# A state-space and expert-routing kernel on one core: the last mixer batch is projected in two parts, and the last layer's rows are gathered with an add

## The chip, the cores and the metric

One core of a Trainium2 chip runs the whole program. The metric is the device time of one execution in microseconds (us). Five engines run instruction streams of their own and meet at semaphores: TensorE (PE), VectorE (DVE), ScalarE (ACT), GpSimd (POOL) and SyncE (SP). The two that issue DMAs here are SP (plain copies) and POOL (gathers by an index, and copies that add into their destination). All of them share the core's 16 DMA engines.

## What is computed

Three layers over x of 8 batches x 2048 tokens x 256 features, all in fp32 (the biases, weights and index tables are left out here):

```
x = x + 0.5 * ffn(layernorm(x))      # first expert layer
x = x + mixer(layernorm(x))          # state-space layer
x = x + 0.5 * ffn(layernorm(x))      # last expert layer
# ffn: gate by 8 Sinkhorn rounds, each of 8 experts takes its 256 best tokens,
#      out[token] = gate * x[token] @ W_expert; of several experts the highest-numbered stands
# mixer: xr = x @ W_in.T; x_conv = silu(conv4(xr[:512])); delta = softplus(x_conv)
#      h[t] = exp(-delta * A) * h[t-1] + x_conv^2      (16 states for each of 512 channels)
#      y = x_conv * sum(h) * silu(xr[512:]) + D * x_conv;   out = y @ W_out.T
```

## The kernel before, in words

The program has four stages: `route` (normalise the rows of x, gates, top 256 tokens), `mixer`, `route` again on the mixer's result, and `ffn`. The first expert layer is computed inside `mixer`, one batch ahead of the state-space layer.

**`mixer`.** Channels go in four units of 128 (J = 4), each with 16 states (N = 16), so that a batch has 64 steps q = 0 to 63. At a step ACT makes the decay exp(delta * neg_a) in a state buffer (L1341), DVE scans it over 2048 tokens (L1143), and after each odd step POOL issues a DMA that adds the even step's state into the odd one's (L1034). PE then sums the pair into four PSUM banks `ps_sum` through an identity matmul (L1555), sixteen states in eight pairs. When a unit's eight pairs are in, DVE multiplies the sum with the gate (`gate`, L1116) and forms the unit's y (`combine`, L1124). The output projection y @ W_out.T (`project_out`, L1523) needs all four units. For a batch b it runs in eight pieces r, spread over the steps of batch b + 1: PE projects 2 x 128 tokens over the four units into a PSUM bank, ACT copies it to a `rows_out` buffer (`copy_out`, L1275), and POOL adds it to x2 in HBM by DMA (`add_result`, L1018), 256 KB each. For the last batch there is no next one to hide it: after all scans the eight pieces run one after the other. SP waits for all adds (the waits on `x2_added`), and only then does the second `route` start.

**`ffn`.** A batch is sixteen slots (`SL` = 16; two per expert, 128 tokens each). For a slot POOL gathers 128 normalised rows (`f_picked`, L1716), PE turns them (L1798), DVE copies them out of PSUM (L1754), PE applies the expert (L1805), ACT scales by the gate (L1784), and SP stores the result to `routed_rows` (L1690). When all sixteen slots of batch m are stored, POOL gathers the result back in token order, sixteen gathers of 128 rows (`f_back`, L1728), and DVE adds each into `total[m % 2]`, which holds the batch's x (L1769). SP stores `total` to the output (L1697) and loads x of a later batch into it (`load_x`, L1683). The order of the work is written out in "rounds" b of slots s. Each engine takes round b, slot s in turn, and the lags are constants:

```
NX = NY = NK = 8
BRING, JOIN, LOAD = SL + 6, SL + 10, 3
if s == LOAD and there(b - 1) and there(b - 3):          # SP: wait out_stored, then load_x(b - 1)
if s == JOIN - SL + 2 and there(b - 2):                  # SP: wait added, then store out of b - 2
m, t = behind(b, s, BRING)                               # POOL: gather back t of batch m, 22 slots after slot t
m, t = behind(b, s, JOIN)                                # DVE: add gather t, 26 slots after slot t; at t == 0 wait x_in
```

So in round b POOL starts the gathers back of batch b - 1 behind the pick of slot 6, SP loads the x of batch b - 1 once slot 3 of round b is scaled and stored, and DVE first needs that x at slot 10. Each ring has eight buffers: POOL's pick of slot s waits until slot s - 8 is turned, its gather back t until DVE has added t - 8, ACT's scaling until the store eight slots before has landed. The x of batches 0 and 1 is loaded at the start of the stage.

## Time and profile before

| | us |
|---|---|
| median of 3 runs | 3737.79 (3731.17 to 3739.79) |
| the profiled execution, its time | 3728.65 |
| its span | 3727.1 |
| DVE busy in the span | 3116.6 (84%) |
| PE busy | 2784.6 (75%) |
| ACT busy | 2123.0 (57%) |
| POOL busy | 1322.5 (35%) |
| granted PE clock, mean | 0.86 |

Busy shares are of the whole span. The stages have different limits: the mixer, to about 2950 us, keeps DVE at its scans, and the last expert layer, from about 3316 us, has no engine that is busy all the time. So the places are read one by one: the stretch between the last scan and the second `route`, and the rounds of the last layer.

### The profile page before, as it was taken

The page shows a single profiled execution, that of the slowest core. Times are in us where ns is not written, and L with a number is a line of the kernel's source. Part 1 is how long each engine was busy: PE and PEld are TensorE (multiplying, and loading weights), DVE is VectorE, ACT ScalarE, POOL GpSimd, SP SyncE. Part 2 cuts the span into 40 slices and gives each one's busy share as a digit, 9 for nine tenths or more (in the row PEclk, how much of TensorE's full clock was granted, in tenths as well). Part 3 has the DMA queues.
Part 4 walks back from the last instruction along what each step waited for, and adds up shares of the span by engine and source line. Part 5 has one row for each costly group of instructions (what it writes and reads, how often), then busy time and mean ns, then how long its engine had stood idle before and what let it go on. Part 6 is the DMA issues. An engine that isn't in the chain of part 4 may idle for free. (4 is left out here: it accounts for less than half of the span.)

```text
span 3727.1 us, 29733 instructions
## 1 busy us (share of the span) xinstructions
PE 2784.6 (75%) x9244; PEld 1530.2 (41%) x9244; DVE 3116.6 (84%) x2640; ACT 2123.0 (57%) x2277; POOL 1322.5 (35%) x897
## 2 busy tenths in 40 slices
PE   8703688899889799889988978987896687025653
PEld 4502333354345346435434534633442445024442
DVE  6797579999999999999999999999999566982222
ACT  6301467876877877787687787777767263001111
POOL 0002254436345344443734534450111100025665
PEclk9655799999999999999999989999998896557776
DMA  7202277688678778868867878886776462034666
GB/s 275 105 0 85 72 179 178 145 181 183 150 163 168 174 173 167 183 145 182 185 150 162 167 170 173 169 178 121 141 144 123 86 257 108 0 109 130 224 219 243
DMA packets 146619, 574.71 MB, mean 154 GB/s; under 512 B 22144, under 2 KB 73920, under 8 KB 99776
## 3 DMA queue, kind: packets, MB, share of 16 engines
q0 software_dynamic: 77136, 399.56, 51.6%
q1 hardware_dynamic: 69360, 173.68, 12.7%
q8 instruction: 55, 0.90, 0.1%
q14 instruction: 68, 0.56, 0.0%
HBM read 154.72 MB, written 117.51 MB: 73 GB/s over the span
## 5 line engine op out<-in xcount | busy, mean ns | idle before, releaser
L1143 DVE TENSOR_TENSOR_SCAN state<-state,drive 128x2048 f32<-128x2048 f32 x512 | 2224.3, 4404 | 54.0 <-ACT state L1341 53.7
L1341 ACT ACTIVATE state<-delta,neg_a 128x2048 f32<-128x2048 f32 x512 | 1019.4, 2005 | 230.3 <-DMA state<-state 95.7
L1555 PE MATMUL ps_states<-state,ident 128*128 128x512 f32 x1800 | 856.4, 621 | 109.5 <-DMA state<-state 94.8
L1034 POOL DMA_DIRECT2D state<-state x256 | 234.9, 919 | 1314.1 <-DVE state L1143 1303.7
L1491 PE MATMUL ps_proj<-x1t,w_in 128*128 128x512 f32 x1024 | 505.0, 637 | 90.6 <-ACT xc L1290 32.3
L1555 PEld LDWEIGHTS ps_states<-state,ident 128*128 128x128 f32 x1800 | 348.7, 200 | 516.5 <-issue 385.5
L1507 PE MATMUL ps_proj<-conv_in,tap 128*128 128x512 f32 x1024 | 488.1, 628 | 53.9 <-ACT conv_in L1262 33.0
L982 POOL DMA_INDIRECT picked<-normed_rows,slot_now x112 | 355.9, 3178 | 99.1 <-PE ps_rows L1472 55.0
L998 POOL DMA_INDIRECT x<-routed_rows,row_now x112 | 345.3, 3083 | 34.6 <-issue 34.6
L1491 PEld LDWEIGHTS ps_proj<-x1t,w_in 128*128 128x128 f32 x1024 | 202.8, 203 | 369.6 <-issue 265.8
L1507 PEld LDWEIGHTS ps_proj<-conv_in,tap 128*128 128x128 f32 x1024 | 203.8, 202 | 319.2 <-issue 280.3
L1754 DVE COPY f_picked_t<-f_ps_turn 128x256 f32<-128x256 f32 x128 | 54.1, 424 | 258.2 <-DMA picked<-normed_rows,slot_now 115.3
L1805 PE MATMUL f_ps_out<-f_expert,f_picked_t 128*128 128x256 f32 x512 | 184.5, 499 | 91.1 <-DVE f_picked_t L1754 55.2
L1784 ACT ACTIVATE f_routed<-f_ps_out,slot_gate 128x256 f32<-128x256 f32 x128 | 60.4, 474 | 316.8 <-PE f_ps_out L1805 136.1
L1523 PE MATMUL ps_rows<-w_out,xc 128*128 128x256 f32 x768 | 204.6, 391 | 5.0 <-DVE xc L1124 5.0
L1716 POOL DMA_INDIRECT f_picked<-normed_rows,f_slot_now x128 | 131.2, 1025 | 199.1 <-issue 189.1
L1523 PEld LDWEIGHTS ps_rows<-w_out,xc 128*128 128x128 f32 x768 | 188.6, 306 | 19.6 <-issue 7.2
L1269 ACT COPY delta<-ps_proj 128x512 f32<-128x512 f32 x124 | 72.1, 583 | 213.3 <-PE ps_proj L1507 213.2
L1805 PEld LDWEIGHTS f_ps_out<-f_expert,f_picked_t 128*128 128x128 f32 x512 | 118.6, 255 | 117.9 <-DVE f_picked_t L1754 61.7
L1728 POOL DMA_INDIRECT f_back<-routed_rows,f_row_now x128 | 122.5, 957 | 101.2 <-DVE f_total L1769 53.3
L1464 PE MATMUL ps_rows<-expert,picked_t 128*128 128x256 f32 x448 | 116.1, 382 | 5.0 <-ACT picked_t L1227 5.0
L1275 ACT COPY rows_out<-ps_rows 128x512 f32<-128x512 f32 x64 | 37.6, 587 | 136.7 <-PE ps_rows L1523 124.3
(288 smaller groups left out, 3233.9 us busy)
## 6 DMA issues: line engine op xcount, KB each, us to landing
state<-state POOLq DMA_DIRECT2D x256, 1024.0 KB, 7.1
delta<-xc POOLq DMA_DIRECT2D x24, 1024.0 KB
normed_rows<-rows_in SPq DMA_DIRECT2D x8, 2048.0 KB
x_rows<-x SPq DMA_DIRECT2D x16, 1024.0 KB, 7.4
x_rows<-rows_out POOLq DMA_DIRECT2D x64, 256.0 KB, 8.3
normed_rows<-rows_mid SPq DMA_DIRECT2D x8, 2048.0 KB
f_total<-x_rows SPq DMA_DIRECT2D x8, 2048.0 KB
routed_rows<-f_routed SPq DMA_DIRECT2D x128, 128.0 KB
```

Source lines behind the costliest of these rows:

```text
L982: nc.gpsimd.indirect_dma_start(out=picked[s % NX][:], out_offset=None, in_=g.normed, in_offset=bass.IndirectOffsetOnAxis(ap=slot_now[:, s: ...
L998: nc.gpsimd.indirect_dma_start(out=x1[:, t, :], out_offset=None, in_=g.routed[0], in_offset=bass.IndirectOffsetOnAxis(ap=row_now[:, t:t + ...
L1034: nc.gpsimd.dma_start(out=state[held(q)][:], in_=state[held(q - 1)][:], accum_op=ALU.add).then_inc(pair_landed(b, q // 2)[0], 16)
L1143: nc.vector.tensor_tensor_scan(state[held(q)][:], state[held(q)][:], drive[j % 2][:], 0.0, ALU.mult, ALU.add).then_inc(state_ready, 1)
L1341: nc.scalar.activation(state[held(q)][:], delta[j % 2][:], ACT.Exp, scale=g.neg_a[:, j, n:n + 1]).then_inc(decay_ready, 1)
L1491: mm = nc.tensor.matmul(ps_proj[bank][:], g.w_in[:, k, col:col + P], x1t[:, k, c * CH:(c + 1) * CH], start=(k == 0), stop=(k == KD - 1))
L1507: mm = nc.tensor.matmul(ps_proj[c % 2][:], tap[:, j * KC + k, :], conv_in[:, c * CH + k:c * CH + k + CH], start=(k == 0), stop=(k == KC - 1))
L1523: mm = nc.tensor.matmul(out_bank(r, last)[:, (t % 2) * D:(t % 2 + 1) * D], y_now[j].rearrange("p (n t) -> p n t", t=T)[:, :, t], g.w_out[: ...
L1555: mm = nc.tensor.matmul(ps_sum[c][:], g.ident[:], state[held(q)][:, c * CH:(c + 1) * CH], start=(opening and n == 1), stop=(n == N - 1))
L1716: nc.gpsimd.indirect_dma_start(out=picked[s % NX][:], out_offset=None, in_=g.normed, in_offset=bass.IndirectOffsetOnAxis(ap=slot_now[b % 2 ...
L1728: nc.gpsimd.indirect_dma_start(out=back[t % NK][:], out_offset=None, in_=g.routed[m], in_offset=bass.IndirectOffsetOnAxis(ap=row_now[m % 2 ...
L1805: mm = nc.tensor.matmul(ps_out[s % NT4][:, 0:D], picked_t[s % NT4][:, k, :], expert[:, s // NH, k, :], start=(k == 0), stop=(k == KD - 1))
```

## The change

There are two parts, in two stages.

**Mixer, last batch only.** The eight pieces of the output projection are done in two parts. Pieces k = 0 to 7 project units 0 to 2 during the fourth unit's steps (PE at steps 55, 57, 59 and 61, ACT's copies at 59, 61, 62 and 63, into `x1`), and POOL adds them to x2 in two DMAs of 1 MB (`add_first_units`, behind steps 61 and 63). Pieces 8 to 15 project unit 3 alone after the scans, are copied into the two `delta` buffers, and are added by four DMAs of 512 KB (`add_last_unit`). The last pair of states is not added by DMA any more: PE sums the states of steps 62 and 63 each by itself (`add_state`), and DVE's last `gate` begins bank by bank.

**Last expert layer.** The gather back adds into `total` by itself (`compute_op=ALU.add`), so DVE's add and the `back` buffers are gone. POOL waits for x (`x_in`) at gather 0 of a batch, and the wait for `added` is gone. The rings for picks and results have sixteen buffers. SP's store of the output moves from slot 12 to slot 10 of its round and waits for the gathers.

The diff, cut to its core:

```diff
@@ mixer @@
+    END = NB - 1
+    END_PUT = {55: (0, 1, 2), 57: (3, 4), 59: (5, 6), 61: (7,)}
+    END_COPY = {59: (0, 1), 61: (2,), 62: (3,), 63: (4, 5, 6, 7)}
+    END_ADD = {61: 0, 63: 1}
...
         for i in range(NOUT):
-            sp.wait_ge(x2_added[i], NB * 16 * (GO // NOUT))
+            sp.wait_ge(x2_added[i], (NB - 1) * 16 * (GO // NOUT))
+        sp.wait_ge(end_out, 4 * 16)
...
+        def add_first_units(i):
+
+            pool.wait_ge(x1_stored[0], NB * 16)
+            pool.wait_ge(x1_stored[1], NB * 16)
+            pool.wait_ge(end_copied, (i + 1) * G2 // 2)
+            pool.sem_inc(g.passed_pool, 1)
+            nc.gpsimd.dma_start(out=x2_v[END, :, i * TH:(i + 1) * TH, :], in_=x1[:, i * TH:(i + 1) * TH, :],
+                                accum_op=ALU.add).then_inc(end_added[i], 16)
+
+        def add_last_unit(i):
+
+            pool.wait_ge(end_added[i // 2], 16)
+            pool.wait_ge(end_copied, G2 + 2 * (i + 1))
+            pool.sem_inc(g.passed_pool, 1)
+            nc.gpsimd.dma_start(out=x2_v[END, :, 4 * i:4 * i + 4, :],
+                                in_=delta[i // 2][:, i % 2 * 4 * D:(i % 2 + 1) * 4 * D].rearrange("p (t d) -> p t d", t=4),
+                                accum_op=ALU.add).then_inc(end_out, 16)
...
             for q in range(1, J * N, 2):
-                pool.wait_ge(state_ready, b * J * N + q + 1)
...
+                if not last or q < J * N - 1:
+                    pool.wait_ge(state_ready, b * J * N + q + 1)
...
+                if last and q in END_ADD:
+                    add_first_units(END_ADD[q])
...
         batches(pool, body)
-        for i in range(GO):
-            add_result(NB - 1, i)
+        for i in range(4):
+            add_last_unit(i)
...
         def gate(b, j):
-            dve.wait_ge(pair_used, sums_taken(b, (j + 1) * (N // 2) - 1))
+            last = isinstance(b, int) and u == NB * J - 1
+            if not last:
+                dve.wait_ge(pair_used, sums_taken(b, (j + 1) * (N // 2) - 1))
             dve.wait_ge(res_gated, u + 1)
             for c in range(C):
+                if last:
+                    dve.wait_ge(end_summed, c + 1)
...
+        def copy_end(k):
+            if k == 0:
+                act.wait_ge(x1_stored[0], NB * 16)
+                act.wait_ge(x1_stored[1], NB * 16)
+            act.wait_ge(end_done, k + 1)
+            nc.scalar.copy(end_rows(k), ps_rows[1 - k % 2][:]).then_inc(end_copied, 1)
...
+        def add_state(q):
+            pe.wait_ge(state_ready, END * J * N + q + 1)
+            for c in range(C):
+                mm = nc.tensor.matmul(ps_sum[c][:], g.ident[:], state[held(q)][:, c * CH:(c + 1) * CH],
+                                      start=False, stop=(q == J * N - 1))
...
+        def project_end(k):
+            if k == 0:
+                pe.wait_ge(y_done, END * J + 3)
...
+            if k == G2:
+                pe.wait_ge(y_done, END * J + 4)
+            pe.wait_ge(end_copied, count(k - 1))
+            r, units = k % G2, (range(J - 1) if k < G2 else (J - 1,))
...
+                    if last:
+                        for r in END_PUT.get(q, ()):
+                            project_end(r)
+                        if q == J * N - 3:
+                            add_state(q + 1)
+                        if q == J * N - 1:
+                            add_state(q)
+                            continue
@@ ffn @@
-    NX = NY = NK = 8
+    NX = NY = SL
...
-    BRING, JOIN, LOAD = SL + 6, SL + 10, 3
+    BRING, STORE, LOAD = SL + 6, SL + 10, 3
...
-                if s == JOIN - SL + 2 and there(b - 2):
-                    sp.wait_ge(added, (b - 1) * T)
+                if s == STORE - SL and there(b - 2):
+                    sp.wait_ge(joined[b % 2], b // 2 * 16 * T)
...
                     if t == 0:
                         pool.wait_ge(rows_set, m + 1)
+                        pool.wait_ge(x_in[m % 2], (m // 2 + 1) * 16)
                         for k in range(NY):
                             pool.wait_ge(routed_out[k], (m + 1) * 16 * (SL // NY))
-                    pool.wait_ge(added, count(m * T + t - NK + 1))
...
-                        out=back[t % NK][:], out_offset=None, in_=g.routed[m],
+                        out=total[m % 2][:, t, :], out_offset=None, in_=g.routed[m],
...
+                        compute_op=ALU.add).then_inc(joined[m % 2], 16)
...
-                m, t = behind(b, s, JOIN)
-                if there(m):
-                    if t == 0:
-                        dve.wait_ge(x_in[m % 2], (m // 2 + 1) * 16)
-                    dve.wait_ge(back_in[t % NK], (m * (T // NK) + t // NK + 1) * 16)
-                    nc.vector.tensor_tensor(total[m % 2][:, t, :], total[m % 2][:, t, :], back[t % NK][:], ALU.add
```

How the change moves instructions at the end of the mixer, on PE. Before, from the fourth unit's opening to the first projections of the last batch (L1546 opens the sums, L1555 sums a pair, L1523 projects; a row's x counts like matmuls in a row):

```order
L1546 MATMUL ps_states<-ones 128x512 x4
L1555 MATMUL ps_states<-state,ident 128x512 x28
L1523 MATMUL ps_rows<-w_out,xc 128x256
L1523 MATMUL ps_rows<-w_out,res 128x256
L1523 MATMUL ps_rows<-w_out,xc 128x256 x3
```

And now, the last part of the same stretch (L1586 is `project_end`, L1639 sums a pair, L1569 is `add_state`):

```order
L1639 MATMUL ps_states<-state,ident 128x512 x4
L1586 MATMUL ps_rows<-w_out,xc 128x256
L1586 MATMUL ps_rows<-w_out,res 128x256
L1586 MATMUL ps_rows<-w_out,xc 128x256 x2
L1586 MATMUL ps_rows<-w_out,res 128x256
L1586 MATMUL ps_rows<-w_out,xc 128x256
L1569 MATMUL ps_states<-state,ident 128x512 x4
L1639 MATMUL ps_states<-state,ident 128x512 x4
L1569 MATMUL ps_states<-state,ident 128x512 x4
L1586 MATMUL ps_rows<-w_out,xc 128x256 x16
```

Three quarters of the projection stand before the last sums, and sixteen matmuls of 256 columns are left behind them instead of 64.

In the last layer, SP's order of issues, before (L1690 stores a slot, L1683 loads x, L1697 stores the output):

```order
L1690 DMA routed_rows<-f_routed 128x256 x45
L1697 DMA out<-f_total 128x4096
L1690 DMA routed_rows<-f_routed 128x256 x7
L1683 DMA f_total<-x_rows 128x4096
L1690 DMA routed_rows<-f_routed 128x256 x9
```

And now:

```order
L1773 DMA routed_rows<-f_routed 128x256 x43
L1780 DMA out<-f_total 128x4096
L1773 DMA routed_rows<-f_routed 128x256 x9
L1766 DMA f_total<-x_rows 128x4096
L1773 DMA routed_rows<-f_routed 128x256 x7
```

The store of the output comes two slots earlier. The load of x stays where it was, behind the store of slot 3, while its first user is now POOL behind the pick of slot 6.

## Rows read from the trace of the kernel before

**Rows 1.** Busy time by stretch at the mixer's end (x: instructions; PEclk: granted clock).
```profile
2920.00:2931.00 11.00, 4.38 (x9) 1.94 (x10) 11.00 (x3) 0.00 (x0) 0.85 (x1) 0.96 0.54 109
2945.00:2988.00 43.00, 30.92 (x128) 29.69 (x128) 4.18 (x5) 4.69 (x8) 6.84 (x8) 0.88 0.35 49
```
**Rows 2.** Timeline of DVE, last unit (start, us, what, idle before and releaser).
```profile
2892.42 38.94 DVE L1143 TENSOR_TENSOR_SCAN state<-state,drive 128x2048 f32<-128x2048 f32 x9
2944.35 2.48 DVE L1116 TENSOR_TENSOR xc<-ps_states,xc 128x512 f32<-128x512 f32 x4 [12.99 <-PE ps_states L1555]
2946.87 2.35 DVE L1124 SCALAR_TENSOR_TENSOR xc<-xc,skip 128x2048 f32<-128x2048 f32 x1
```
**Rows 3.** Timeline of PE, last sums and first projection (durations at two clocks).
```profile
2893.73 3.70 PE L1555 MATMUL ps_states<-state,ident 128*128 128x512 f32 x8 [2.95 <-DMA state<-state]
...
2938.91 5.40 PE L1555 MATMUL ps_states<-state,ident 128*128 128x512 f32 x8 [3.36 <-DMA state<-state]
2949.28 1.23 PE L1523 MATMUL ps_rows<-w_out,xc 128*128 128x256 f32 x2 [4.96 <-DVE xc L1124]
```
**Rows 4.** Timeline of ACT, the last piece's copy.
```profile
2980.24 0.59 ACT L1275 COPY rows_out<-ps_rows 128x512 f32<-128x512 f32 x1 [2.98 <-PE ps_rows L1523]
```
**Rows 5.** Timeline of all engines where the mixer ends and `route` starts.
```profile
2981.50 0.86 POOL L1018 DMA_DIRECT2D x_rows<-rows_out  x1 [2.81 <-ACT rows_out L1275]
2988.11 1.76 SPq L221 DMA_DIRECT2D rows_mid<-x_rows  x4
```
**Rows 6.** DMA issues from 2940 to 2990 us (KB each, median us to landing).
```profile
x_rows<-rows_out POOLq DMA_DIRECT2D x8, 256.0 KB, 4.1
```
**Rows 7.** Busy time by stretch of the last layer, cut at each batch's first gather back.
```profile
3366.10:3414.00 47.90, 28.39 (x108) 20.97 (x106) 10.99 (x31) 7.95 (x17) 30.37 (x33) 0.71 0.47 132
...
3652.90:3697.70 44.80, 20.48 (x74) 15.52 (x74) 12.54 (x35) 6.53 (x14) 23.90 (x25) 0.74 0.67 219
3697.70:3727.10 29.40, 0.00 (x0) 0.00 (x0) 6.79 (x17) 0.00 (x0) 15.51 (x16) 0.50 0.70 274
```
**Rows 8.** Timeline of POOL, one round: the picks of slots 3 and 6, gathers back.
```profile
3497.70 0.94 POOL L1716 DMA_INDIRECT f_picked<-normed_rows,f_slot_now x1 [0.30 <-issue]
...
3505.22 0.95 POOL L1716 DMA_INDIRECT f_picked<-normed_rows,f_slot_now x1 [0.30 <-issue]
3510.59 0.95 POOL L1728 DMA_INDIRECT f_back<-routed_rows,f_row_now x1 [4.42 <-DVE f_total L1769]
```
**Rows 9.** Groups of POOL's instructions, 3366 to 3698 us (idle before, releasers).
```profile
L1728 POOL DMA_INDIRECT f_back<-routed_rows,f_row_now x113 | 107.9, 955 | 96.3 <-DVE f_total L1769 53.3 <-issue 32.9 <-PE f_ps_turn L1798 5.0
```
**Rows 10.** Timeline of SP in the last layer (SPq: its DMA queue).
```profile
3514.50 0.43 SPq L1683 DMA_DIRECT2D f_total<-x_rows  x1
...
3606.88 0.42 SPq L1683 DMA_DIRECT2D f_total<-x_rows  x1
...
3694.31 0.33 SPq L1683 DMA_DIRECT2D f_total<-x_rows  x1
3698.28 22.44 SPq L1697 DMA_DIRECT2D out<-f_total  x2
```
**Rows 11.** Chain of waits, two gathers of picks, start and us to landing.
```profile
3415.21 2.94 DMA f_picked<-normed_rows,f_slot_now
...
3514.35 8.04 DMA f_picked<-normed_rows,f_slot_now
```
**Rows 12.** Timeline of PE, one slot's expert matmuls and one turn.
```profile
3525.93 1.91 PE L1805 MATMUL f_ps_out<-f_expert,f_picked_t 128*128 128x256 f32 x4
3527.64 0.63 PE L1798 MATMUL f_ps_turn<-ident,f_picked 128*128 128x128 f32 x2
```
**Rows 13.** Busy time by stretch while the x of a batch is loaded.
```profile
3612.00:3614.00 2.00, 0.00 (x0) 0.00 (x0) 0.76 (x2) 0.00 (x0) 1.63 (x2) 0.50 1.03 418
3616.00:3618.00 2.00, 1.89 (x6) 1.62 (x7) 0.00 (x0) 0.47 (x1) 1.39 (x2) 0.50 0.72 270
```
**Rows 14.** Timeline of DVE, the first add of batch 7.
```profile
3705.53 0.43 DVE L1769 TENSOR_TENSOR f_total<-f_total,f_back 128x256 f32<-128x256 f32 x1 [7.28 <-DMA f_back<-routed_rows,f_row_now]
```

More of the change, by code:

```diff
@@ L796, in mixer @@
     x2_added = [sem(f"x2_added{i}") for i in range(NOUT)]
+    end_done, end_copied, end_summed, end_out = (sem(n) for n in ("end_done", "end_copied", "end_summed", "end_out"))
+    end_added = [sem(f"end_added{i}") for i in range(2)]
     x_v = x.rearrange("b (p t) d -> b p t d", t=T)
@@ L1031, in body @@
             for q in range(1, J * N, 2):
-                pool.wait_ge(state_ready, b * J * N + q + 1)
-                pool.sem_inc(g.passed_pool, 1)
-                nc.gpsimd.dma_start(out=state[held(q)][:], in_=state[held(q - 1)][:], accum_op=ALU.add
-                                    ).then_inc(pair_landed(b, q // 2)[0], 16)
+                if not last or q < J * N - 1:
+                    pool.wait_ge(state_ready, b * J * N + q + 1)
+                    pool.sem_inc(g.passed_pool, 1)
+                    nc.gpsimd.dma_start(out=state[held(q)][:], in_=state[held(q - 1)][:], accum_op=ALU.add
+                                        ).then_inc(pair_landed(b, q // 2)[0], 16)
+                if last and q in END_ADD:
+                    add_first_units(END_ADD[q])
                 for r in range(G2):
@@ L1352, in body @@
                         decay(b, q, first)
+                    if last:
+                        for k in END_COPY.get(q, ()):
+                            copy_end(k)
                     if n == BEGIN[j] and (j or not first):
@@ L1644, in ffn @@
     routed = [sb(f"f_routed{i}", [P, D]) for i in range(NY)]
-    back = [sb(f"f_back{i}", [P, D]) for i in range(NK)]
     total = [sb(f"f_total{i}", [P, T, D]) for i in range(2)]
@@ L1651, in ffn @@
     routed_out = [sem(f"f_routed_out{i}") for i in range(NY)]
-    back_in = [sem(f"f_back_in{i}") for i in range(NK)]
+    joined = [sem(f"f_joined{i}") for i in range(2)]
     x_in = [sem(f"f_x_in{i}") for i in range(2)]
     out_stored = [sem(f"f_out_stored{i}") for i in range(2)]
-    turned, copied, product, scaled, added = (
-        sem(n) for n in ("f_turned", "f_copied", "f_product", "f_scaled", "f_added"))
+    turned, copied, product, scaled = (
+        sem(n) for n in ("f_turned", "f_copied", "f_product", "f_scaled"))
     table = RankTable(ints=[sb(f"f_token_i{i}", [P, R * NH], I32)[:] for i in range(2)],
@@ L1743, in set_rows @@
         def set_rows(b):
-            for k in range(NK):
-                dve.wait_ge(back_in[k], count((b - 1) * 16 * (T // NK)))
+            if b >= 2:
+                dve.wait_ge(joined[b % 2], b // 2 * 16 * T)
             nc.vector.tensor_copy(row_now[b % 2][:], g.token_row[:, b, :]
```

24 lines of the change are left out of this document (19 added, 5 removed).

## The prediction

> **What bounds the kernel now.** The profiled execution took 3728.65 us over a span of 3727.1 and lies 9 us under the median of the runs, 3737.79. I make the sum against that execution and carry the difference over to the median. I read the busy times by stretch first, then the timelines at the two places that the change touches.
>
> *The mixer's end.* DVE scans without a gap to 2931.36 [rows 2]. Then it waits 13 us: the last pair is added by DMA, PE sums it from 2938.91 to 2944.31, DVE gates for 2.48 and combines for 2.35, and PE projects from 2949.28 [rows 2, 3]. The eight pieces take 3.57 each (a 0.59 copy and 2.98 of waiting for PE [rows 4]). POOL issues the last add at 2981.50, it lands in about 4.1, and `route` starts at 2988.11 [rows 5, 6]. So 57 us lie between the last scan and the next stage with nothing beside them, and every microsecond cut there is a microsecond of the total.
>
> *The last layer.* No engine is always busy: in the stretch from 3652.9 to 3697.7 PE works 20.5 of 44.8 us, POOL 23.9, and DMA has a share of 0.67 [rows 7]. POOL is the nearest to a bound, since a gather costs it 0.95 and the next starts 1.25 later [rows 8]: 32 gathers make 40.1 us a batch. From the first gather back of batch 0 (3366.1) to that of batch 7 (3697.7) it took 331.6 us for seven batches, 47.4 each [rows 7]. The difference is mostly POOL waiting for DVE's add to free one of eight buffers, 53.3 us in all [rows 9], 4.42 in the round shown [rows 8].
>
> **The mixer's end, part by part.** A sum of a pair (eight instructions) costs PE 3.70 at full clock and 5.40 at the lower one [rows 3]. A piece of 16 instructions takes 3.57, so one instruction 0.223. The first-part pieces have 12 (2.7), the second-part pieces 4 (0.9). From the end of the sum at 2897.4 [rows 3] PE now has eight first-part pieces (21.4) and six sums (pairs 27 to 30, and states 62 and 63 singly; 22.2): it is done at 2941.0, after the last scan. That is 3.3 before 2944.31. The gate now runs bank by bank beside the last sum, so only its last quarter (0.6) is left of 2.48, another 1.9. This is 5.2 in all. At the lower clock the six sums would cost 10 more. The clock granted there was 0.96 [rows 1] and PE will be fuller, so I take 1 off: 4.2 earlier, and the second part starts at about 2945.1.
>
> What are the scans' risks? ACT's eight new copies (0.59 each) stand behind decays of steps 59 to 63, which ACT makes well ahead of DVE. PE's sums come later by some pieces, and the decay of step 63 needs the sum of pair 27, now at about 2909.5, while its scan is due at 2927. I charge nothing. If that cover were gone, each late scan would cost what it is late by. The two adds of 1 MB go out behind the last state add and before the second part. They cost the path nothing unless they delay the last pair, which PE takes up only after a first-part piece and a sum.
>
> The second part is eight pieces of 0.9 (7.2), with adds of 512 KB after each two. The adds are what is late next. DMA engines moved adds of 8 KB per partition at 109 GB/s with a share of 0.54, 202 GB/s when busy, and adds of 2 KB at 49 with 0.35, 140 GB/s [rows 1]. These adds have 4 KB, between the two: 185 GB/s, 2.8 us each, bounds 2.6 and 3.7. The first is issued after two pieces and a copy, at 2947.8. Four transfers take 11.2, and the rest of a landing is 2.2 (4.1 less 1.9 for 256 KB at 140 [rows 6]): 2961.2. `route` follows 2.5 after the landing, as before (2981.50 + 4.1 to 2988.11 [rows 5, 6]): 2963.7 in place of 2988.1. **Gain 24.4**, between 18 (slow adds, PE at the lower clock) and 27.
>
> The Trainium skill (DMA: Bandwidth & Descriptors, Anatomy of one DMA) fits any POOL-issued DMA by 2.0 us + bytes at 436 GB/s, without a dearer case for adds. By that figure four adds would take 4.8 us, less than PE's pace, and the end would come 3 us sooner. The rows show adds at under half that rate, so they decide.
>
> **The last layer, part by part.** DVE's 128 adds and POOL's waits for them go: 53.3 us of POOL's idle time. What takes their place is the wait for x. SP loads the x of batch b - 1 in round b, behind slot 3's store. DVE needed it at slot 10, but POOL now wants it behind the pick of slot 6, and everything on POOL is queued behind that wait, so picks stop and then PE. In the round shown the pick of slot 3 was issued at 3497.70, that of slot 6 at 3505.22, and the load of x only at 3514.50 [rows 8, 10]: POOL would stand there before the load has even been issued.
>
> So a batch's period is now a loop. From a first gather back to the next round's pick of slot 3 POOL issues 25 gathers: 31.3 us. Then slot 3 must be scaled. PE turns slot 4 first, so: 2.5 until that pick, 2.9 for its landing on quiet queues [rows 11], 0.6 turn, 1.9 expert [rows 12], 0.6 scaling (at most a copy of twice the size [rows 4]) and 0.3 of hand-overs, 8.8. A burst of 2 MB makes picks late (8.04 beside the load issued at 3514.50, against 2.94 [rows 10, 11]). The store of the output is such a burst, some slots earlier in the round, and I add 1.9 for what is left of it: 10.7. Two issues by SP: 0.9. The landing of 2 MB: the load issued at 3606.88 kept the DMA engines full until about 3616.5, 9.6 us, beside gathers [rows 10, 13]. The last store of 2 MB, alone, took 6.4 (3720.72 to the end at 3727.1 [rows 7, 10]). With POOL standing still the load is nearly alone: 7.8. With 0.3 to wake POOL the period is 31.3 + 10.7 + 0.9 + 7.8 + 0.3 = **51.0**, against 47.4.
>
> This holds for five of the seven periods. The x of batch 1 is there from the start, so the first is POOL's own 40.1. In the last, no picks follow: 21.3 to the pick of slot 15, 11 to its scaling beside a burst, 0.9, and 9.5 to the landing, as the output store follows at once (11.2 with one beside it in the trace, 3694.31 to 3705.53 [rows 10, 14]): 43. Sum 40.1 + 255 + 43 = 338.1 against 331.6, **6.5 lost**, and 0.7 at the end, where a gather that adds lands later but DVE's last add of 0.43 goes.
>
> The gathers that add have no row. For POOL's time the bounds are a gather, 0.95, and half again as much, 1.4; a direct add costs it 0.86 [rows 5], less than a gather, so I take 0.95. For the DMA engines: at 140 to 185 GB/s the adds of a batch take 11 to 15 us and the rest some 23 (load, store, slot stores and picks), under 51, so they do not bind. The rings of sixteen add nothing by themselves: once POOL stops at slot 6 it cannot be more than seven picks ahead. SP's store of the output, now at slot 10, waits for gathers that POOL issued by slot 5, and costs nothing. The second `route` and the other layers are untouched.
>
> **Sum.** -24.4 + 6.5 + 0.7 = -17.2: 3711 for an execution like the profiled one, and 3737.8 - 17.2 = **3721** for the median.
>
> **The rivals.** (a) *The wait for x is much longer, and the kernel is slower.* In the trace slot 3 took 16.8 from its pick to the load (3497.70 to 3514.50). If that stays, with 9.5 for the landing, the period is 58.8 and the layer loses 40.1 + 294 + 45 - 331.6 = 47.5 more: 3738 - 24 + 48 = 3762. It decides from a period of 55. For it speaks the measured row; against it that part of those 16.8 is backlog of bursts, which empties while POOL stands still. 0.13. The Trainium skill (DMA: Bandwidth & Descriptors, Rules for kernel authors) says that an accumulating DMA must wait for the earlier DMA on the same bytes, so this wait cannot simply be dropped. By that rule the time is (a)'s or mine, according to the load.
> (b) *Between.* A period of 53 to 56 eats the mixer's gain: within 7.5 of the median. 0.12.
> (c) *The loop is short.* No backlog (8.8) and 6.8 for a load alone: period 48.1, 14.5 better than forecast: 3706. With the mixer's upper end, 3703. 0.10.
> (d) *The gathers do not add at a gather's price.* At 1.4 on POOL 13 of the 25 gathers cost 0.45 more, 6 us a period, 41 in all: 3762 too. 0.05.
> (e) *The mixer's end gives only 18*, by slow adds or late scans: 3727. This is inside my own case.
>
> **How the numbers follow.** 0.60 for the forecast (3708 to 3730), 0.10 for (c), 0.12 for (b), 0.18 for (a) and (d). About 0.2%, 7.5 us, is what a measurement of this kernel can tell from no change. Faster takes the first two and a sliver of (b): 0.72. Same 0.11, slower 0.17. The range leaves out the far half of (a) and (d) and the far end of (c): 3702 to 3748.
>
> **What would show it.** `route`'s first load at about 2964; PE's second part from 2945; scans as dense as before; the first x-wait of POOL at batch 2, 8 to 14 us long each, five times; no DVE add; gathers that add at 0.95 on POOL; distances of 40 once, then 51. A period under 45 or an `x_in` wait that is missing makes the second half of the argument wrong; a first load after 2972 the first.

## The result, and the profile after

The changed kernel took **3791.28 us** (median of 4 runs, 3786.41 to 3795.9) beside 3734.48 us for the kernel before (4 runs, 3729.42 to 3739.79). The ratio is 1.0155, 95% interval 1.0133 to 1.0177: 57 us slower. Forecast were 3721 us and a range up to 3748. The profiled execution took 3795.9 us over a span of 3794.0, the highest of the four, while that of the kernel before (3728.65) was below all of its runs; so the two spans are 66.9 us apart and the medians 57.

| part of the span, us | before | after | difference |
|---|---|---|---|
| start to the end of the last scan | 2931.4 | 2938.6 | +7.3 |
| last scan to the first load of the second `route` | 56.7 | 34.1 | -22.7 |
| from there to the first pick of the last layer | 328.0 | 327.6 | -0.4 |
| first pick to the first gather back | 50.0 | 59.9 | +9.9 |
| seven periods, first gather back of batch 0 to that of batch 7 | 331.6 | 395.6 | +64.0 |
| from there to the end | 29.4 | 38.2 | +8.8 |

The first line is no effect of the change. The stretch is the same but for the last batch's end, and in the 18 traces of the runs below, of kernels that differ only behind it or only in this end, it ended anywhere from 2920 to 2940 us.

**The mixer's end.** Timeline of DVE, last unit:

```profile
2899.69 38.94 DVE L1182 TENSOR_TENSOR_SCAN state<-state,drive 128x2048 f32<-128x2048 f32 x9
2945.51 1.48 DVE L1155 TENSOR_TENSOR xc<-ps_states,xc 128x512 f32<-128x512 f32 x2 [6.88 <-PE ps_states L1569]
...
2948.01 0.69 DVE L1155 TENSOR_TENSOR xc<-ps_states,xc 128x512 f32<-128x512 f32 x1 [0.17 <-PE ps_states L1569]
2948.74 2.35 DVE L1163 SCALAR_TENSOR_TENSOR xc<-xc,skip 128x2048 f32<-128x2048 f32 x1
```

The nine scans last 38.94 us without a gap, exactly as in [rows 2]: the copies and the sums held up none. DVE's wait behind them is 6.9 us, before 13. On PE the sums of state 62, pair 30 and state 63 stand back to back at a granted clock of 1.00, and after DVE's combine 32 matmuls are left:

```profile
2937.51 3.60 PE L1569 MATMUL ps_states<-state,ident 128*128 128x512 f32 x8
2940.95 3.60 PE L1639 MATMUL ps_states<-state,ident 128*128 128x512 f32 x8
2944.38 3.60 PE L1569 MATMUL ps_states<-state,ident 128*128 128x512 f32 x8
2951.15 9.41 PE L1586 MATMUL ps_rows<-w_out,xc 128*128 128x256 f32 x32 [3.17 <-DVE xc L1163]
```

Timelines of POOL and SP, from the first of the four adds to `route`'s first load:

```profile
2955.88 0.86 POOL L1049 DMA_DIRECT2D x_rows<-delta  x1 [16.03 <-ACT delta L1323]
...
2961.75 0.86 POOL L1049 DMA_DIRECT2D x_rows<-delta  x1 [1.07 <-issue]
...
2972.69 1.76 SPq L221 DMA_DIRECT2D rows_mid<-x_rows  x4
```

**The last layer.** Busy time by stretch, the first period, the second, and the end (they answer to [rows 7]; behind the length come the busy times of PE, of PE's weight loads, of DVE, ACT and POOL, each with its number of instructions, then the granted clock, the busy share of the DMA engines and GB/s):

```profile
3360.20:3410.50 50.30, 33.98 (x109) 22.60 (x108) 7.97 (x21) 8.81 (x19) 40.52 (x33) 0.68 0.62 131
3410.50:3470.00 59.50, 35.44 (x106) 23.16 (x104) 7.78 (x20) 8.52 (x18) 40.46 (x33) 0.61 0.71 185
...
3755.80:3794.00 38.20, 0.00 (x0) 0.00 (x0) 0.00 (x0) 0.00 (x0) 24.65 (x16) 0.50 0.66 165
```

POOL now works 40.5 us in a period, where it worked 30.4 [rows 7]. One round on POOL's timeline (compare [rows 8]): the first gather back of batch 1 and the pick behind it, then the picks of slots 3 and 6 of the next round, the gather that waits for x, and the one that waits in the round after:

```profile
3410.49 1.55 POOL L1811 DMA_INDIRECT f_total<-routed_rows,f_row_now  x1 [0.30 <-issue]
3412.34 0.98 POOL L1799 DMA_INDIRECT f_picked<-normed_rows,f_slot_now  x1 [0.31 <-issue]
...
3450.01 0.98 POOL L1799 DMA_INDIRECT f_picked<-normed_rows,f_slot_now  x1 [0.30 <-issue]
...
3459.41 0.98 POOL L1799 DMA_INDIRECT f_picked<-normed_rows,f_slot_now  x1 [0.30 <-issue]
3469.99 1.55 POOL L1811 DMA_INDIRECT f_total<-routed_rows,f_row_now  x1 [9.59 <-issue]
...
3530.02 1.55 POOL L1811 DMA_INDIRECT f_total<-routed_rows,f_row_now  x1 [10.15 <-issue]
```

And SP's timeline, where the loads of x stand (compare [rows 10]):

```profile
3460.04 0.43 SPq L1766 DMA_DIRECT2D f_total<-x_rows  x1
...
3519.09 0.46 SPq L1766 DMA_DIRECT2D f_total<-x_rows  x1
```

Two things are to be read here. **A gather that adds costs POOL 1.55 us and not 0.95**, so a pair of a gather back and a pick takes 1.85 + 1.28 = 3.13 us instead of 2.50. **And POOL stands still for about 10 us** until x has landed. (The profile names the load only at the last of these waits, of 7.95 us before 3755.80; that the others are the same is shown by the run with x loaded earlier, below.) The loop of the forecast is there: from 3410.49 to the pick of slot 3 it took 39.5 us, from that to the load 10.0, and from the load to POOL's next gather, at 3469.99, 9.95: together the 59.5 of this period.

### The profile page after: what moved, and what is told of

The parts are those of the page before. It is cut to its first block and busy times, and to the rows that moved or that the text cites. A ratio compares the mean times of both kernels' runs of the same rounds, so it can differ in the third digit from the quotient of the medians.

```text
span 3794.0 us, 29636 instructions
## 1 busy us (share of the span) xinstructions
PE 2825.3 (74%) x9252; PEld 1542.6 (41%) x9252; DVE 3074.4 (81%) x2512; ACT 2127.4 (56%) x2285; POOL 1390.7 (37%) x894
## 3 DMA queue, kind: packets, MB, share of 16 engines
q0 software_dynamic: 88992, 400.61, 52.5%
## 5 line engine op out<-in xcount | busy, mean ns | idle before, releaser
L1639 PE MATMUL ps_states<-state,ident 128*128 128x512 f32 x1792 | 849.5, 619 | 83.1 <-DMA state<-state 66.2
L1639 PEld LDWEIGHTS ps_states<-state,ident 128*128 128x128 f32 x1792 | 346.5, 199 | 484.0 <-issue 383.5
L1811 POOL DMA_INDIRECT f_total<-routed_rows,f_row_now x128 | 197.9, 1546 | 113.7 <-issue 82.5
L1874 PE MATMUL f_ps_turn<-ident,f_picked 128*128 128x128 f32 x256 | 75.7, 392 | 177.7 <-DMA f_picked<-normed_rows,f_slot_now 175.3
L1881 PE MATMUL f_ps_out<-f_expert,f_picked_t 128*128 128x256 f32 x512 | 201.6, 539 | 6.6 <-DVE f_picked_t L1837 6.6
L1599 PE MATMUL ps_rows<-w_out,xc 128*128 128x256 f32 x672 | 178.5, 388 | 0.1
L1599 PEld LDWEIGHTS ps_rows<-w_out,xc 128*128 128x128 f32 x672 | 164.9, 305 | 13.1 <-issue 7.2
L1881 PEld LDWEIGHTS f_ps_out<-f_expert,f_picked_t 128*128 128x128 f32 x512 | 132.7, 284 | 25.2 <-DVE f_picked_t L1837 7.3
L1874 PEld LDWEIGHTS f_ps_turn<-ident,f_picked 128*128 128x128 f32 x256 | 36.1, 184 | 238.7 <-DMA f_picked<-normed_rows,f_slot_now 208.2
```

The source lines that it names most:

```text
L1599: mm = nc.tensor.matmul(out_bank(r, last)[:, (t % 2) * D:(t % 2 + 1) * D], y_now[j].rearrange("p (n t) -> p n t", t=T)[:, :, t], g.w_out[: ...
L1639: mm = nc.tensor.matmul(ps_sum[c][:], g.ident[:], state[held(q)][:, c * CH:(c + 1) * CH], start=(opening and n == 1), stop=(n == N - 1))
L1811: nc.gpsimd.indirect_dma_start(out=total[m % 2][:, t, :], out_offset=None, in_=g.routed[m], in_offset=bass.IndirectOffsetOnAxis(ap=row_now ...
L1881: mm = nc.tensor.matmul(ps_out[s % NT4][:, 0:D], picked_t[s % NT4][:, k, :], expert[:, s // NH, k, :], start=(k == 0), stop=(k == KD - 1))
```

## The experiments

There are eighteen runs of nine kernels, in five sets, each set with its own runs of the kernel before. These came out in two kinds: 3666 to 3667 us in three sets (here the *quicker* sets: a, c and d) and 3724 to 3725 us in two (the *slower* sets: b and e). The first result, with 3734 us, is like the slower ones. The expectations speak of two kinds of chip. That the kind belongs to the chip is not shown: the record gives b, a slower set, and d, a quicker one, the same chip number, 8. Ratios hold within a set. "Start" is the time from the first pick of the last layer to the first gather back, "period" that from one batch's first gather back to the next's. "Mixer's end alone" is the changed `mixer` with the `ffn` of before.

### Set a: the parts of the change (before: 3667.27 us)

**Mixer's end alone.**

> The mixer's end of the change on the last layer of before. Price theory (the loss is all in the last layer: a gather that adds costs POOL 1.55 us where a plain one costs 0.95, and POOL waits for x): 22 to 24 us faster than before, about 3712; first load of the second route 34 us after the last scan (56.8 before). Rival (the denser end of the mixer delays scans or the following stage, part of the loss is from there): gain under 12 us.

3640.79 us, ratio 0.9926 (0.9908 to 0.9943), 26 us faster. From the last scan to `route` 32.9 us. The periods were 40.2 to 41.9 but for the last, 34.1: in this set POOL waits only 2.7 us in all for DVE's adds, and 32 gathers at 1.25 us are the bound. Groups of POOL's and PE's instructions, 3330 to 3610 us (idle before, releasers):

```profile
L1889 PE MATMUL f_ps_out<-f_expert,f_picked_t 128*128 128x256 f32 x438 | 142.1, 460 | 0.4 <-DVE f_picked_t L1838 0.3
L1812 POOL DMA_INDIRECT f_back<-routed_rows,f_row_now x114 | 110.3, 968 | 43.0 <-issue 26.8 <-PE f_ps_turn L1882 10.3 <-DMA routed_rows<-f_routed 3.2
```

Of the 53.3 us of waiting for DVE's add that [rows 9] show hardly any is there.

**Rings of sixteen alone** (kernel before):

```diff
-    NX = NY = NK = 8
+    NX = NY = SL
+    NK = 8
```

> Before, with sixteen buffers instead of eight for the last layer's picks and results, nothing else. Price theory: rings of sixteen change little, within 5 us of before, since POOL waits for DVE's adds and not for picks. Flood rival (deeper rings let 23 gathers run at once, fill the DMA queues and delay the first batch): first gather back 60 us after the first pick instead of 50.0, 8 to 12 us slower.

3668.61 us, ratio 0.9998 (0.9986 to 1.0011), start 50.2, periods of 40.1 to 40.7 and 36.2 for the last. Here the rings neither help nor cost.

**The changed kernel with rings of eight.**

```diff
-    NX = NY = SL
+    NX = NY = 8
```

> The changed kernel with rings of eight again. Price theory: periods stay at 59 to 60 us and the time is within 5 us of the changed kernel's 3791. Flood rival: the first batch is back at 50 us from pick to gather back (59.9 with sixteen) and the time is 10 us or more below the changed kernel's.

3773.78 us, ratio 1.028 (1.0258 to 1.0302). Periods 50.3, 59.2 to 61.1 five times, 49.3, as in the changed kernel's first profile. So the loss of the periods does not come from the rings. In this set the whole loss is 133 us against the mixer's end alone. The start was 50.1 us, and 49.5 in the next run with rings of sixteen, so in this set they do not delay it either. The periods of the kernel with plain gathers depend on the set (40 or 47), those of this one don't.

**The changed kernel with x loaded earlier**, behind slot 14 of the round before:

```diff
-    BRING, STORE, LOAD = SL + 6, SL + 10, 3
+    BRING, STORE, LOAD = SL + 6, SL + 10, 14
...
-                if s == LOAD and there(b - 1) and there(b - 3):
-                    sp.wait_ge(out_stored[(b - 1) % 2], (b - 1) // 2 * 16)
-                    load_x(b - 1)
+                if s == LOAD and there(b) and there(b - 2):
+                    sp.wait_ge(out_stored[b % 2], b // 2 * 16)
+                    load_x(b)
```

> The changed kernel with the x of batch b loaded behind slot 14 of round b, five slots of SP's order earlier than now, so that it is in HBM-to-SBUF flight before POOL needs it. Loop theory: POOL's waits of 8 to 10 us at a batch's first gather back go, six of them, and the periods fall from 59.5 to POOL's own 16 x (1.28 + 1.85) = 50.2: 45 to 55 us below the changed kernel, 3736 to 3746. Rival (the DMA queues are the bound, the wait only shows them): periods stay above 56.

3730.13 us, ratio 1.0164 (1.0146 to 1.0183): 43.7 us less than the run before it, which had rings of eight. Six periods of 50.2 to 50.3, then 48.4. That is POOL's own time, 16 x 1.85 + 16 x 1.28 = 50.1. The wait for x is gone from the groups of POOL (3340 to 3690 us), which now read

```profile
L1811 POOL DMA_INDIRECT f_total<-routed_rows,f_row_now x113 | 174.8, 1547 | 57.7 <-issue 30.2 <-PE f_ps_turn L1874 18.8 <-DMA routed_rows<-f_routed 8.8
L1799 POOL DMA_INDIRECT f_picked<-normed_rows,f_slot_now x105 | 102.9, 980 | 32.0 <-issue 31.4 <-PE f_ps_turn L1874 0.3 <-DMA routed_rows<-f_routed 0.3
```

against 109.1 us of idle time before the same 113 gathers in the changed kernel. So the two causes part cleanly in this set: the wait for x is worth 9 to 10 us a period, and the dearer gathers another 10 (50.2 against 40.2).

### Set b: the price of a gather that adds (before: 3724.65 us)

**The changed kernel, again.**

> The changed kernel itself, beside the others on one chip. If the price of a gather that adds (1.55 us on POOL) and the wait for x make the loss, its last layer has the periods of the first profile again, 59 to 60 us, and it stands 45 to 60 us above the kernel that loads x early. The start of 59.9 us from the first pick to the first gather back: if rings of sixteen make it, it comes again; if it was a chance of that execution, it is 50.

3790.8 us, ratio 1.0169 (1.0141 to 1.0198). Start 58.5, periods 50.3, 58.9 to 60.1 five times, 47.7: the first result, repeated.

**Half of the gathers add.** As the run with the early load (here behind slot 15), but odd gathers go plain into eight `back` buffers, with an add on DVE:

```diff
+                    if t % 2:
+                        nc.gpsimd.indirect_dma_start(
+                            out=back[t // 2][:], out_offset=None, in_=g.routed[m],
...
+                    if t % 2:
+                        dve.wait_ge(back_in[t // 2], (m + 1) * 16)
+                        nc.vector.tensor_tensor(total[m % 2][:, t, :], total[m % 2][:, t, :], back[t // 2][:], ALU.add
```

> The changed kernel with x loaded behind slot 15, and only the even gathers back adding by DMA; the odd ones are plain, into eight buffers, and DVE adds them (the output store goes back to slot 12). Price theory (POOL pays 0.6 us more for each gather that adds, whatever else): periods 16 x 1.28 + 8 x 1.85 + 8 x 1.25 = 45.3 us, half way between 40.1 and 50.2, about 35 us below the kernel with all gathers adding and x early. Rival (the dearer gathers come from the traffic of adds or from DVE being away, not from the instruction): the plain gathers rise too or the adding ones fall, and the period is not half way.

3730.09 us, ratio 1.0016 (0.9996 to 1.0037), so the mixer's gain is given back here too. In one kernel, side by side, the gathers that add took 1.59 us and the plain ones 0.96 (POOL's groups, 3340 to 3690 us):

```profile
L1823 POOL DMA_INDIRECT f_total<-routed_rows,f_row_now x57 | 90.8, 1593 | 67.5 <-issue 25.9 <-PE f_ps_turn L1896 22.5 <-DMA routed_rows<-f_routed 10.5
L1818 POOL DMA_INDIRECT f_back<-routed_rows,f_row_now x57 | 54.8, 962 | 17.4 <-issue 15.8 <-DVE f_total L1867 0.9 <-PE f_ps_turn L1896 0.3
```

The rival falls, since the price goes with the instruction. POOL's own time would give 16 x 1.28 + 8 x 1.89 + 8 x 1.26 = 45.7 a period. It took 45.5 to 56.0; what lies above 45.7 is not POOL's price (more on the slower sets below). The 35 us expected against the kernel with all gathers adding cannot be read, since that ran in set a.

**The price by rows.** Of each four gathers back one adds 128 rows, one adds 64, one brings 128 and one 64 (half of the gathers then leave out 64 rows, and the plain ones are not added, so that part of the result is missing):

```diff
+                    n = P // 2 if t % 2 else P
+                    if t % 4 < 2:
+                        nc.gpsimd.indirect_dma_start(
+                            out=total[m % 2][0:n, t, :], out_offset=None, in_=g.routed[m],
```

> A look at what POOL pays for: in the changed kernel with x early, gathers back alternate between four kinds: adding 128 rows, adding 64 rows, plain 128 rows, plain 64 rows. It leaves out the other 64 rows of every second gather and does not add the plain ones. If POOL works row by row when it adds (one packet for each row, where a plain gather has one for four), 64 rows cost about 1.1 us against 1.55, and the plain ones differ less, about 0.8 against 0.95. If adding has a fixed price, 64 rows with the add cost 0.6 more than 64 plain ones.

POOL's timeline, the four kinds in a row (a pick stands between each two):

```profile
3512.72 1.56 POOL L1816 DMA_INDIRECT f_total<-routed_rows,f_row_now  x1 [3.58 <-DMA routed_rows<-f_routed]
...
3515.88 1.42 POOL L1816 DMA_INDIRECT f_total<-routed_rows,f_row_now  x1 [0.30 <-issue]
...
3518.89 0.95 POOL L1821 DMA_INDIRECT f_back<-routed_rows,f_row_now  x1 [0.30 <-issue]
...
3521.40 0.90 POOL L1821 DMA_INDIRECT f_back<-routed_rows,f_row_now  x1 [0.30 <-PE f_ps_turn L1884]
```

To add costs 0.61 us more for 128 rows and 0.52 for 64. Most of it belongs to the instruction, not to its rows, so gathers of fewer rows would not save it. (The run took 3744.46 us, once, which says little, since it leaves work out.)

**Mixer's end, plain gathers, early load and deep rings.**

```diff
-    NX = NY = NK = 8
+    NX = NY = NK = SL
-    BRING, JOIN, LOAD = SL + 6, SL + 10, 3
+    BRING, JOIN, LOAD = SL + 6, SL + 10, 15
```

with `load_x(b)` as above.

> The mixer's end of the change, and in the last layer plain gathers with DVE's adds, but sixteen buffers in all three rings and x loaded behind slot 15. POOL theory: the last layer cannot go under 40.1 us a batch, so where the kernel before has that already (as on the chip of the last runs) it is as fast as the mixer's end alone, ratio 0.992 to 0.994 to before; where before has periods of 47 us it gains up to 45 us more, ratio down to 0.981. Rival (bursts hold POOL up whatever the rings are): no more than the mixer's end on either.

3773.47 us, ratio 1.0118 (1.0095 to 1.0141), **slower**, though nothing adds by DMA: start 61.6, periods of 56.5 to 59.5 and 46.8 for the last. This missed both the expectation and its rival: it is slower than before by 49 us. Sets c and d look into it.

### Sets c and d: rings and early load apart (before: 3666.29 and 3666.99 us)

> The mixer's end of the change alone, again, since the chips differ: on the chip of the first look the kernel before ran its batches of the last layer in about 47 us, on another in 40.2. If the gain of the mixer's end is its own, it is 20 to 27 us here too whatever the periods are (ratio 0.993 to 0.995). If it is given back where the periods are 47, the ratio is 0.998 or more.

3644.36 us, ratio 0.9934 (0.9922 to 0.9946).

> The changed kernel with rings of eight. On the chip where it ran before, it took 50.1 us from the first pick to the first gather back, and the changed kernel with rings of sixteen took 58.5 to 59.9 on two others. If the rings of sixteen let more transfers be under way at the start and so delay the first gather back, this kernel takes 50 us there on any chip. If it is the chip, it takes 58 or more here where the kernel before has periods of 47. The periods stay at 59 to 60 either way.

3768.22 us, ratio 1.0276 (1.0262 to 1.0289), start 49.5, long periods of 58.1 to 60.3.

> The kernel before with sixteen buffers of picked and of routed rows. On a chip with periods of 40.2 it was as fast as before (0.9998). If deep rings cost nothing by themselves, the ratio is 0.999 to 1.001 here too; if they lengthen the transfers where these are slower, the first gather back comes 58 instead of 50 us after the first pick, and the ratio is 1.002 or more.

3669.01 us, ratio 1.0002 (0.9993 to 1.0011), start 50.0.

> The mixer's end of the change, the plain gathers with adds on VectorE and rings of eight, and only the load of x moved to the end of the round before (the run with this and rings of sixteen took 1.0118 of the time before, with periods of 56 to 59). If the rings of sixteen made that run slow, this one is as fast as the mixer's end alone (0.992 to 0.995). If the early load of x did, it is slow as well, above 1.005.

3645.7 us, ratio 0.9943 (0.993 to 0.9955), periods of 40.1 to 40.8 but the last. This was a quicker set, so it could not speak of the slower kind. Set d came out quicker as well:

> The mixer's end alone, on whatever chip this is. On two chips where the kernel before takes 3666 to 3667 us it took 0.9926 and 0.9934 of that. If the gain is its own, 0.993 to 0.995 also where the kernel before takes 3725 or more; if the gain is given back there, 0.998 or more.

3642.76 us, ratio 0.9947 (0.993 to 0.9964).

> The changed kernel with rings of eight. If rings of sixteen cause the late start of the last layer, the first gather back comes 50 us after the first pick on every chip; if it is the chip's own, 58 or more where the kernel before takes 3725 us or more. The periods stay 59 to 60 either way.

3772.71 us, ratio 1.0284 (1.0265 to 1.0302), start 50.2.

> Mixer's end, early load of x, rings of eight. If the early load made the run with deep rings slow, the ratio is above 1.005 where the kernel before takes 3725 us or more; if the rings did, 0.992 to 0.996.

3643.27 us, ratio 0.9938 (0.9922 to 0.9955).

> Mixer's end, early load of x, and rings of sixteen for picked, routed and gathered rows, plain gathers. It took 1.0118 of the time before on the chip with 3725 us. If its slowness belongs to the rings whatever the chip, above 1.005 here too, with periods of 56 or more; if it needs a chip of the slower kind, 0.992 to 0.996 with periods of 40 to 41 where the kernel before takes 3667 us.

3644.18 us, ratio 0.9944 (0.9927 to 0.9961), start 51.8, periods of 40.2 to 40.7 but the last. This is the kernel that took 1.0118 in set b. So the early load and the deep rings cost nothing in a quicker set, and 1.0118 needs the slower kind. The same two groups show where the time is; first set d's (3333 to 3616 us), then set b's (3356 to 3752 us):

```profile
L1889 PE MATMUL f_ps_out<-f_expert,f_picked_t 128*128 128x256 f32 x441 | 141.9, 457 | 0.1
L1812 POOL DMA_INDIRECT f_back<-routed_rows,f_row_now x116 | 112.0, 965 | 58.1 <-issue 30.2 <-PE f_ps_turn L1882 20.1 <-DVE f_total L1853 6.0
```

```profile
L1889 PE MATMUL f_ps_out<-f_expert,f_picked_t 128*128 128x256 f32 x438 | 154.6, 490 | 174.2 <-issue 128.8 <-DVE f_picked_t L1838 45.4
L1812 POOL DMA_INDIRECT f_back<-routed_rows,f_row_now x113 | 107.6, 952 | 179.7 <-PE f_ps_turn L1882 82.3 <-DVE f_total L1853 50.9 <-issue 31.4
```

POOL's cost per gather is the same (0.97 and 0.95); in set b PE and POOL wait. It is not that PE lacks picked rows. The groups of its turns, in the same two stretches, set d's first:

```profile
L1882 PE MATMUL f_ps_turn<-ident,f_picked 128*128 128x128 f32 x218 | 56.1, 348 | 99.7 <-DMA f_picked<-normed_rows,f_slot_now 99.1 <-DVE f_picked_t L1838 0.5
```

```profile
L1882 PE MATMUL f_ps_turn<-ident,f_picked 128*128 128x128 f32 x216 | 51.9, 335 | 38.4 <-DMA f_picked<-normed_rows,f_slot_now 25.6 <-issue 12.8
```

For picks PE waited 99.1 us in the quicker set and only 25.6 in the slower. What is new in the slower one is 128.8 us that the profile puts down to "issue" before the expert matmuls: time for which it shows no wait. The first profile of the kernel before and the mixer's end alone in set e have it too (35.9 and 56.7 us in the seven periods), the mixer's end alone in set d has none. The landing times are mostly missing from the slower traces; the one that both have, a slot's store of 128 KB, is 3.7 us in set b and 2.6 in set d (medians of the two runs).

### Set e: the slower kind again (before: 3723.84 us)

> The mixer's end alone: 0.993 to 0.995 where the kernel before takes 3666 us; where it takes 3725 or more, 0.993 to 0.996 if the gain is its own, and 0.998 or more if it is given back.

3705.14 us, ratio 0.9946 (0.9925 to 0.9967). The gain is kept where a period takes 46 to 50 us too.

> The changed kernel with rings of eight: 1.028 where the kernel before takes 3666 us. Where it takes 3725 or more: first gather back 50 us after the first pick and a ratio near 1.013 if the rings of sixteen cause the late start there, 58 us or more and 1.0155 if the chip does.

3779.28 us, ratio 1.0156 (1.0136 to 1.0177), start 50.5, long periods of 58.4 to 60.1. The changed kernel, with rings of sixteen, started in 59.9 and 58.5 us in slower sets, and three others with rings of sixteen in 56.5 (half adds), 59.5 (price by rows) and 61.6 (deep rings); all that had rings of eight there started in 50.0 (before, mixer's end alone) or 50.5. In the quicker sets the start was 49.5 to 51.8 with either. So the late start goes with the rings of sixteen, and only in the slower kind: five traces against three. Two kernels that differ in nothing but their rings never ran side by side in a slower set, though, and the kernel before with deeper rings alone never ran in one. The ratios (1.0169 and 1.0156, of different sets) are too close to show these 8 us; the traces do. What it looks like, by stretch of 5 us behind the first pick: the changed kernel in its first profile,

```profile
3320.30:3325.30 5.00, 0.56 (x4) 0.42 (x4) 0.00 (x0) 0.00 (x0) 3.78 (x5) 0.50 0.52 171
3325.30:3330.30 5.00, 0.87 (x3) 0.23 (x2) 0.53 (x2) 0.47 (x1) 1.23 (x2) 0.50 0.22 70
```

and the same place in the run of set e with the mixer's end alone and rings of eight:

```profile
3317.40:3322.40 5.00, 3.65 (x44) 2.63 (x44) 5.00 (x7) 0.90 (x3) 3.50 (x4) 1.00 0.71 231
3322.40:3327.40 5.00, 3.55 (x44) 2.62 (x44) 5.00 (x7) 0.74 (x3) 3.70 (x3) 1.00 0.32 99
```

With rings of sixteen POOL issues the last of the sixteen picks of batch 0 and goes on, while PE, DVE and ACT all but stop for 10 us and the DMA engines are busy to 0.52 and then 0.22. With eight POOL is held back by PE's turns, and PE keeps its pace. The timelines of PE, DVE and ACT in the first of the two show more:

```profile
3317.16 0.42 PE L1874 MATMUL f_ps_turn<-ident,f_picked 128*128 128x128 f32 x2
3317.41 1.03 PE L1881 MATMUL f_ps_out<-f_expert,f_picked_t 128*128 128x256 f32 x4
...
3320.53 0.17 PE L671 MATMUL f_ps_turn<-f_at_tile,f_at_part 128*128 128x16 bf16 x1 [1.81 <-issue]
```

```profile
3318.32 0.17 DVE L1823 COPY f_slot_now<-slot_token 128x16 int32<-128x16 int32 x1
3329.78 0.42 DVE L1837 COPY f_picked_t<-f_ps_turn 128x256 f32<-128x256 f32 x1 [11.29 <-DMA x<-in_x]
```

```profile
3329.83 0.47 ACT L1860 ACTIVATE f_routed<-f_ps_out,slot_gate 128x256 f32<-128x256 f32 x1 [12.41 <-DMA state<-normed_rows,slot_token]
```

PE had turned slot 3 by 3317.58 and DVE copied it only at 3329.78. PE had finished slot 2's expert by 3318.44 and ACT scaled it only at 3329.83. The waits that the program puts before these two were met by then, and the DMAs that the profile names as releasers are of earlier stages. In the run of set e the second of these two copies follows the first after 0.01 us. So this stall is no wait for gathered rows. What holds the engines is not shown, nor why it goes with more gathers under way.

## Why the prediction was wrong, point by point

- **The mixer's end: right.** Forecast were 24.4 us off the path from the last scan to `route`, within 18 to 27; the trace shows 22.7, and four runs of this part alone were 18.7 to 26.5 us faster than the medians of before in their sets. The scans stayed dense. PE's last sum was expected done 9.6 us behind the last scan and was after 9.3. The second part started 12.5 behind it (forecast 13.7), the first add went out after 17.2 (16.4), and four adds took 3.0 us each by the same sum instead of 2.8. Rival (e) fell. One reading was off without harm: the sum of 5.40 us was not one at the lower clock but at a mixed one (granted 1.00, then 0.57 and 0.65), so six sums wholly at the lower clock would have cost more than the 10 us named. PE's three last sums ran at 1.00, in 3.60 each. And by the forecast's own steps the figure of the Trainium skill would bring the end nearly 5 us sooner, not 3.
- **The loop of the last layer: right in its shape.** POOL waited at the first gather back of batches 2 to 7, five long periods stood between a first short one and a last shorter one, and slot 3 took 10.0 us from its pick to the load, where 11.6 were forecast with SP's two issues. Rival (a) held that this stretch stays at 16.8; it did not, though its period of 58.8 is near the measured 59.3. A right number here came from a wrong reason. The 16.8 themselves were not shown to be a backlog of bursts, as the forecast had it: in them ACT stood idle for 10.91 us at a stretch (of which the profile gives the releaser as "remote", so the cause is open).
- **"So I take 0.95" is the step that failed first.** The step priced a gather that adds like a plain one "since a direct add costs it 0.86, less than a gather", and set the upper bound at 1.4, half again as much. Measured were 1.55, outside both, and 0.03 more for each pick between. The 25 gathers took 39.5 us and not 31.3, the first period 50.3 and not 40.1, the end 38.2 instead of 30.1: 8 in each of five periods, 10 and 8. In the period shown this is nearly the whole error (8.2 of 8.5), since the next two terms, 1.9 too little for the load and 1.6 too much for slot 3, all but cancel. The row of the direct add was no bound: it was of another kind of DMA, without an index.
- **The landing of x, 7.8 us and 0.3 to wake POOL, was mis-sized**: 9.95 in the period shown. The step set it between a load beside gathers (9.6) and a store alone (6.4), and took POOL's standing still for a quiet queue. But gathers that add were issued up to that wait; that they slow the load is likely and not shown. The last period took 48.8 instead of 43.
- **"The rings of sixteen add nothing by themselves" failed**, in the slower kind of set. The argument looked at the rounds, where POOL does stop at slot 6, and not at the start of the layer, where nothing but the ring stops it: 9.9 us. In the quicker sets the step holds (1.0002 and 0.9998).
- **The sum.** Of the 84 us between the forecast change of span (-17.2) and the measured one (+66.9), the five long periods hold 41.5, the first and the last 16, the end 8, the start 10, the mixer's end 2, and the noise of the first 2930 us, with the stretch behind `route`'s first load, 7.
- **The chances.** What came is rival (d), dearer than its own bound of 1.4, on the loop of the forecast; (a) did not come. (d) had 0.05, though it stood on the one price that no row of the trace bounded, and its 3762 us lacked 0.15 us more for each gather and the late start.

The Trainium skill (DMA: Bandwidth & Descriptors, SWDGE vs HWDGE vs iDMA) says that for GpSimd's DMAs a program on its cores builds the descriptors, and that accumulating in a DMA can be had there only. The page gives no price for it; the traces do: the packets in the queue of POOL's DMAs (q0 in the profile) were 88,992 in the changed kernel and 76,704 in the one of set b with plain gathers and the same mixer, 96 more for each of the 128 gathers, and POOL paid 0.6 us more for each. That the packets make the 0.6 is not shown, since half the rows saved only 0.09 of the difference.

**The version to keep** is the mixer's end alone. It beat the kernel before in all four sets in which it ran, three quicker and one slower (0.9926 to 0.9947, upper ends up to 0.9967). The changed kernel, with rings of sixteen or of eight, lost wherever it ran.

## What to carry to other kernels

An operation folded into a transfer need not be free for the engine that issues it. Before an add on an engine with time to spare (DVE, busy to about a third at most in this layer) is moved into a gather, time one such gather beside a plain one: here 0.6 us more, 128 times, on the engine nearest to the bound, to save 0.42 us each on one that was idle for most of the time. When a consumer moves to an earlier place, its input's load must move by as much (44 us in set a). And a term that no row bounds on the upper side deserves more than a chance of 0.05 of being wrong.

## What had not been expected of the hardware

- A gather of 128 rows of 1 KB costs POOL 0.95 us plain and 1.55 with an add; of 64 rows 0.90 and 1.42. A direct add of 256 or 512 KB costs it 0.86.
- The same kernel before took 3666 to 3667 us in three sets of runs and 3724 to 3734 in three others. In the traces of a last layer with plain gathers and rings of eight a period took 40 to 42 us in the one kind and 45 to 51 in the other (the last one less), at the same 0.95 to 0.97 per gather on POOL. The sign of the slower kind in a trace is idle time of PE, DVE and ACT for which the profile shows no wait ("issue") or names a DMA of another stage. Whether it is a property of a chip, or of something that changes with time, stays open. It makes the verdict on the changed kernel 1.028 (rings of eight) or 1.016, with the same periods of 59 to 60.
- In the slower kind, with sixteen gathers under way, PE, DVE and ACT stall at the start of the layer with their inputs ready, while the DMA engines are idle for half of the time and more (shares of 0.52 and 0.22). Whether the picked rows' ring or the results' does it, and whether the early load has a share in the 1.0118 of set b, was not told apart there: the run with the early load and rings of eight came only to quicker sets.
